# Three fused attention layers on one Trainium2 core: a step's projection or turning job placed ahead of the transposes of the probabilities on TensorE

## The chip, the cores and the metric

The kernel runs on one core of one Trainium2 chip. The metric is the device time of one execution in microseconds (us); of the kernel before, the median of 3 runs is 2838.85 us (2832.95 to 2840.29). The engines are called PE (TensorE), DVE (VectorE), ACT (ScalarE), POOL (GpSimd) and SP (SyncE). Each runs its own instruction stream in order; they meet at semaphores only.

## The reference

Four layers act one after the other on x of shape (4, 512, 512) in float32; three of them hold an attention over 512 positions:

```python
# layer 0: 16 heads of 32, q and k normalised per head
x = x + attn(_ln(x) * (scale1 + 1.0) + shift1) * gamma1
x = x + (_gelu_tanh((_ln(x) * (scale2 + 1.0) + shift2) @ Wfc1.T + bfc1) @ Wfc2.T + bfc2) * gamma2
# layer 1: 16 query heads of 32, 4 key heads, latent keys, rotary, a sparse mask
attn = jax.nn.softmax(scores, axis=-1)
y = jnp.einsum('bhts,bhsd->bhtd', attn, v_exp)
x = x + y.transpose(0, 2, 1, 3).reshape(B, T, C) @ Wo.T
# layer 2: 8 query heads of 64, one key head, rotary; then a gated MLP
ctx = jnp.einsum('bkgst,bktd->bkgsd', attn, v)
x = res + ctx @ Wo.T
x = x + (silu(h @ Wg.T) * (h @ Wu.T)) @ Wd.T
# layer 3: 8 experts of width 64, a norm and an output product
```

The change touches the attention of layers 0, 1 and 2 (called l0a, l1a and l2a in the profile), not the MLPs and not layer 3.

## The kernel before

The function `attention` is used for the three layers. A batch element is cut into "steps": step n handles one tile of 128 queries of one head, in the order group of heads (NG groups: 4, 4 and 2), query tile (4), head in the group (4). A group has 16 steps, written s = 0 to 15 below, and a batch element has 64, 64 or 32 steps. The batch elements run one after the other; the two middle ones are one loop on every engine.

The order of the work on each engine is written out by hand in a function `batch` of that engine, and only semaphores tie the engines together. In step n:

- PE multiplies probabilities of a finished query tile by V in one step of four (`weigh`, L835, into psO), computes the scores of step n+2 in l0a and n+1 in l1a and l2a (`scores`, L793 to L799, into psS), transposes the probabilities of step n-6 (`transposes`, L814, four 128x128 transposes in l0a and l2a and one or two in l1a, into one of two banks psT), and runs the step's jobs (`run`, into one of two banks psA).
- DVE takes the row minima of the negated, masked scores of step n (`minima`, L1267 and L1268), which overwrite a slot of `prob`. There are 8 slots, so it waits until PE has transposed the probabilities of step n-8.
- ACT copies the transposed probabilities of step n-7 out of psT (`pT_copy`, L992), takes the exponentials of step n (`exps`, L982), and then empties the psA banks of the jobs of step n-1 (L876, L891, L958, L973, L976 and others). Where n leaves 3 when divided by 4, the exponentials come first and the copy second, and the copy then waits for `weigh`.
- POOL multiplies four tiles of probabilities at a time by the inverse row sums (L1452, L1454).

A job is one of: "proj", "v", "kv", "far", "ck" (projections, L670 and L662), "norm" (transposes of normalised rows, L654), "q" and "k" (the transposes of queries and keys of the next group, L715), and "out" (the output product, L724). The table in `jobs` sets their steps. In l0a the q and k job of one head are both in each of the steps s = 12 to 15, and so fill both banks psA; in l1a there is one q job in each of them and one k job at s = 11, in l2a one q job in each and two k jobs at s = 11. In l0a "proj" stands at s = 2, 4, 6 and 9 (in the third group at s = 10 and 11, in the last group at s = 0 and 1 too), "v" at s = 7 and 8, "norm" at s = 7, 8, 10 and 11 of the third group, and "out" at s = 9, 10 and 11 of the first group and s = 4 of the second.

The two banks psA are taken in turn, whatever the kind of job. Before a job PE waits until the bank was emptied, in `run`:

```python
for w in freed[i]:
    pe.wait_ge(*w)
```

For q and k what it waits for is ACT's copy of the job before last. `transposes` waits for ACT's copy of step m-2 and for POOL's product of step m.

Of the kernel before, what the change touches and what calls it, by code (L numbers as in the profile page):

```python
# [362 lines left out]
def attention(nc, R, D, L, scale_g, shift_g, nxt, fetched=()):  # L363
# [13 lines left out]
    NTILE = 4 * U  # L377
# [14 lines left out]
    with ExitStack() as ctx:  # L392
# [130 lines left out]
        def s_bank(n):  # L523


            n = n % NTILE
            return NS - 2 if n == NTILE - 1 and NTILE % NS else n % NS

        def since(n):

            return next(d for d in range(1, NTILE) if s_bank(n - d) == s_bank(n))
# [62 lines left out]
        def steps(first, more):  # L594

            before = [] if first else [((kind, hg - NG, x), i) for (kind, hg, x), i in banked(first, True, False)[-1]]
            for n, todo in enumerate(banked(first, more, not more)):
                m = n - LAG  # L600
                yield n, todo, before, None if (first and m < 0) or m > NTILE + CL else m
                before = todo

        with nc.Block() as block:
# [42 lines left out]
            def _(pe):  # L647
# [129 lines left out]
                def scores(b, n, first):  # L777
                    u, j = divmod(n, 4)
                    hg, qt = divmod(u, NT)
                    g = b * NG + hg  # L780
                    if qt == 0:
                        pe.wait_ge(qT_done, 4 * g + (j + 1))
                        if is0:
                            pe.wait_ge(kT_done, 4 * g + (j + 1))
                        elif j == 0:
                            pe.wait_ge(kT_done, L.nks * (g + 1))

                    if n >= since(n) or not first:
                        pe.wait_ge(min_done, b * NTILE + (n - since(n) + 1))
                    w = L.width[qt]  # L790
                    q, out = qT[:, j, qt * P:(qt + 1) * P], psS[s_bank(n)][:, 0:w]
                    if is0:
                        mm = pe.matmul(out, q, kT[:, j, 0:w], start=True, stop=True)  # L793
                    elif is1:
                        k0 = P + (qt - 1) * WIN if qt else 0
                        mm = pe.matmul(out, q, kT[:, hg % 2, k0:k0 + w], start=True, stop=True)
                    else:
                        pe.matmul(out, q, kT[:, hg % 2 * 2, 0:w], start=True, stop=False)
                        mm = pe.matmul(out, q, kT[:, hg % 2 * 2 + 1, 0:w], start=False, stop=True)  # L799
                    mm.then_inc(s_done, 1)  # L800
# [5 lines left out]
                def transposes(b, m, first):  # L806

                    if not (first and m < 2):
                        pe.wait_ge(*pT_copied(b, m - 2))
                    pe.wait_ge(p_done, b * NTILE + (m + 1))  # L810
                    qt = m // 4 % NT
                    for c in range(L.parts[qt]):
                        k0 = (FAR if qt and c == 0 else 0) if is1 else c * P
                        mm = pe.transpose(psT[m % 2][:, c * P:(c + 1) * P], prob[:, m % NP, k0:k0 + P], R.ident[:])  # L814
                    mm.then_inc(pT_mm, 1)

                def weigh(b, u, first):

                    hg, qt = divmod(u % U, NT)
                    pe.wait_ge(*pT_copied(b, 4 * u + 3))  # L820
                    if qt == 0:
                        pe.wait_ge(v_done, (b * NG + (u // NT + 1)) * (2 if is0 else 1))
                    if qt == 0 and not (first and u == 0):
                        pe.wait_ge(oh_done, b * NG * NO + u // NT * NO)
                        pe.wait_ge(ol_done, b * NG * NO + u // NT * NO)
                    nk = L.parts[qt]
                    for c in range(nk):
                        for j in range(4):
                            o, row = divmod(j * HD, P)
                            v0 = j * HD if L.nk == 4 else 0  # L830
                            if is1 and c == 1:
                                v, rows = VF[0:FAR, hg % VS, qt - 1, :], FAR
                            else:
                                v, rows = V[:, hg % VS, qt if is1 else c, v0:v0 + HD], P
                            mm = pe.matmul(psO[o][row:row + HD, qt * P:(qt + 1) * P],  # L835
                                           v, PT[0:rows, j, c * P:(c + 1) * P],
                                           start=(c == 0), stop=(c == nk - 1))
                    mm.then_inc(pv_done, 1)

                def batch(b, first, more):  # L840
                    q_k = [(qT_done, 4 * NG * b + 4), (kT_done, L.nks * (NG * b + 1))]
                    freed[0], freed[1] = q_k, q_k
                    for n, todo, _, m in steps(first, more):
                        if m is not None and m % 4 == CL and not (first and m == CL):
                            weigh(b, m // 4 - 1, first)
                        if n + AHEAD < NTILE:
                            scores(b, n + AHEAD, first)
                        elif more and n < NTILE:
                            scores(b + 1, n + AHEAD - NTILE, False)
                        if m is not None and m < NTILE:  # L850
                            transposes(b, m, first)
                        for job, i in todo:
                            run(job, i, b, b + 1, b - 1 if n < NTILE else b)

                for n, job in enumerate(START):
                    if n == NT - PRE:
# [4 lines left out]
                for n in range(AHEAD):  # L861
                    scores(0, n, True)
                batch(0, True, True)
                with pe.Fori(1, B - 1) as b:
                    batch(b, False, True)
                batch(B - 1, False, False)


# [1498 lines left out]
```

## Time and profile before

| | |
|---|---|
| median of 3 runs | 2838.85 us |
| profiled execution | 2829.08 us |
| its span (first to last instruction) | 2827.3 us |
| PE busy | 2401.7 us (85%) |
| DVE busy | 1561.7 us (55%) |
| ACT busy | 1281.9 us (45%) |
| POOL busy | 899.4 us (32%) |
| mean granted clock of PE | 0.908 |

The profiled execution took 1.8 us more than its span and was 9.8 us below the median of the other runs. The steps of l0a lie in the span from about 125 to 770 us, those of l1a from 1213 to 1640 us, and those of l2a from 1683 to 2055 us. The MLPs and the experts lie in between and behind. Busy time counts an engine as busy from the start to the end of an instruction; on PE the ends are modelled, and the next matmul starts before the one before it has ended, so distances between starts are the better measure there.

### The profile page before, as it was taken

The numbers are of one execution on the slowest core, as the hardware profiler recorded it, in microseconds if no ns is written. First come the engines' busy times: TensorE is split into PE (matmuls) and PEld (weight loads), VectorE is DVE, ScalarE is ACT, GpSimd is POOL, SyncE is SP. The second block draws the span as 40 slices with busy tenths as digits, with TensorE's granted clock in tenths as the row PEclk, the third lists the DMA queues.
The fourth block names the chain that finished last, engine by engine and source line by source line (L and its number), as shares of the span: only waits on it lengthen the run. The fifth ranks groups of instructions, "written<-read, shape, count | busy, mean of one in ns | idle before, by whom it ended". The sixth has DMA issues, their size and how long they took to land. (4 is left out here: it accounts for less than half of the span.)

```text
span 2827.3 us, 47254 instructions
## 1 busy us (share of the span) xinstructions
PE 2401.7 (85%) x15668; PEld 1941.5 (69%) x15668; DVE 1561.7 (55%) x4469; ACT 1281.9 (45%) x3183; POOL 899.4 (32%) x988
## 2 busy tenths in 40 slices
PE   3788988898779999678788768989899999996777
PEld 1677777776567888556666557767688888885565
DVE  2777676678564343474565546566553333333866
ACT  1567676766621111276776636566531111112443
POOL 0134333342376767222332312233211212220422
PEclk7899999899889999868778689999999999997898
DMA  5100000000110000110000010000010000001000
GB/s 213 38 2 2 9 2 10 2 2 24 48 43 17 29 30 0 73 61 1 2 1 1 1 41 1 1 1 1 1 68 23 23 23 22 0 0 49 4 27 30
DMA packets 16951, 65.29 MB, mean 23 GB/s; under 512 B 3276, under 2 KB 4044, under 8 KB 11748
## 3 DMA queue, kind: packets, MB, share of 16 engines
q1 hardware_dynamic: 16740, 62.70, 6.3%
q8 instruction: 106, 1.74, 0.3%
q14 instruction: 105, 0.86, 0.1%
HBM read 57.42 MB, written 5.28 MB: 22 GB/s over the span
## 5 line engine op out<-in xcount | busy, mean ns | idle before, releaser
L1830 POOL TENSOR_TENSOR l2m_hidl<-l2m_hid,l2m_hidh 128x512 fp32r<-128x512 f32 x64 | 101.0, 1578 | 447.8 <-DVE l2m_hidh L1800 447.8
L982 ACT ACTIVATE l0a_prob<-l0a_prob,l0a_nmin 128x512 f32<-128x512 f32 x256 | 185.4, 725 | 118.6 <-DVE l0a_nmin L1268 117.3
L1695 ACT ACTIVATE l2m_gate<-l2m_psG 128x512 f32<-128x512 f32 x64 | 38.3, 599 | 437.3 <-PE l2m_psU L1626 436.3
L1452 POOL TENSOR_TENSOR l0a_prob<-l0a_prob,l0a_rinv 128x512 f32<-128x512 f32 x64 | 66.5, 1040 | 517.3 <-DVE l0a_rinv L1275 517.3
L1795 DVE TENSOR_TENSOR l2m_hid<-l2m_gate,l2m_psU 128x512 f32<-128x512 f32 x64 | 44.0, 688 | 282.3 <-ACT l2m_gate L1695 282.3
L992 ACT ACTIVATE l0a_PT<-l0a_psT 128x512 f32<-128x512 f32 x256 | 152.2, 597 | 60.3 <-PE l0a_psO L835 38.9
L1268 DVE CUSTOM_DVE_ANT_0 l0a_prob<-l0a_psS,l0a_mask 128x512 f32<-128x512 f32 x256 | 175.4, 689 | 4.6 <-PE l0a_psS L793 2.9
L1850 POOL TENSOR_TENSOR res_X<-res_X,l0m_share 128x512 f32<-128x512 f32 x128 | 162.8, 1300 | 24.9 <-DVE l0m_share L1784 23.9
L814 PE MATMUL l0a_psT<-res_ident,l0a_prob 128*128 128x128 f32 x1024 | 163.8, 285 | 3.6 <-ACT l0a_PT L992 3.2
L1699 ACT ACTIVATE l0m_hid<-l0m_psG,l0m_b1c 128x512 f32<-128x512 f32 x64 | 43.9, 690 | 265.4 <-PE l0m_psG L1626 265.4
L670 PE MATMUL l0a_psA<-l0a_wh,res_hTh 128*128 128x128 f32 (+1 forms) x512 | 151.2, 295 | 13.4 <-ACT l0a_raw L891 6.2
L793 PE MATMUL l0a_psS<-l0a_kT,l0a_qT 96*128 96x512 f32 x256 | 127.4, 499 | 41.2 <-DVE l0a_nmin L1268 31.4
L814 PEld LDWEIGHTS l0a_psT<-res_ident,l0a_prob 128*128 128x128 f32 x1024 | 134.0, 147 | 27.1 <-ACT l0a_PT L992 6.7
L814 PE MATMUL l1a_psT<-res_ident,l1a_prob 128*128 128x128 f32 x448 | 121.4, 354 | 33.9 <-ACT l1a_PT L992 32.9
L670 PE MATMUL l0a_psA<-l0a_wl,res_hTh 128*128 128x128 f32 (+1 forms) x512 | 145.1, 283 | 0.0
L670 PE MATMUL l0a_psA<-l0a_wh,res_hTl 128*128 128x128 f32 (+1 forms) x512 | 144.8, 283 | 0.0
L1454 POOL TENSOR_SCALAR l0a_prob<-l0a_prob,l0a_rinv 128x512 f32<-128x512 f32 x192 | 140.1, 746 | 0.0
L1452 POOL TENSOR_TENSOR l1a_prob<-l1a_prob,l1a_rinv 128x128 f32<-128x128 f32 (+1 forms) x64 | 32.5, 507 | 327.6 <-DVE l1a_rinv L1275 327.6
L982 ACT ACTIVATE l1a_prob<-l1a_prob,l1a_nmin 128x198 f32<-128x198 f32 (+1 forms) x256 | 114.8, 449 | 47.0 <-DVE l1a_nmin L1268 46.1
L1452 POOL TENSOR_TENSOR l2a_prob<-l2a_prob,l2a_rinv 128x512 f32<-128x512 f32 x32 | 33.9, 1059 | 300.1 <-DVE l2a_rinv L1275 300.1
L1268 DVE CUSTOM_DVE_ANT_0 l1a_prob<-l1a_psS,l1a_mask 128x198 f32<-128x198 f32 (+1 forms) x256 | 86.1, 342 | 76.5 <-issue 71.1
L1268 DVE CUSTOM_DVE_ANT_0 l2a_prob<-l2a_psS,res_zero 128x512 f32<-128x512 f32 x128 | 87.8, 687 | 69.3 <-issue 68.7
(402 smaller groups left out, 7665.7 us busy)
## 6 DMA issues: line engine op xcount, KB each, us to landing
res_l2m_stage<-in_l2m_w SPq DMA_DIRECT2D x8, 1536.0 KB, 6.4
res_l0m_stage<-in_l0m_w SPq DMA_DIRECT2D x8, 1024.0 KB, 4.8
cond_w<-in_wmod SPq DMA_DIRECT2D x6, 1024.0 KB, 7.8
res_X<-in_x SPq DMA_DIRECT2D x4, 1024.0 KB, 9.8
l0a_prob<-in_l0a_w SPq DMA_DIRECT2D x4, 1024.0 KB, 6.6
l1a_wmod<-in_wmod SPq DMA_DIRECT2D x4, 1024.0 KB, 6.1
out<-res_X SPq DMA_DIRECT2D x16, 256.0 KB, 2.0
l_stage<-in_l_w SPq DMA_DIRECT2D x3, 1024.0 KB, 7.2
```

Source lines behind the costliest of these rows:

```text
L670: mm = pe.matmul(ps[:, c0:c0 + n], l[:, k, t * P:(t + 1) * P], cols(r, k), start=(k == 0 and i == 0), stop=(k == NK - 1 and i == 2))
L793: mm = pe.matmul(out, q, kT[:, j, 0:w], start=True, stop=True)
L814: mm = pe.transpose(psT[m % 2][:, c * P:(c + 1) * P], prob[:, m % NP, k0:k0 + P], R.ident[:])
L982: act.activation(prob[:, n % NP, 0:w], src[:, 0:w], ACT.Exp, bias=nmin[:, n % NP:n % NP + 1], scale=-1.0, accum_out=ssum[:, n % NP:n % NP ...
L992: act.activation(PT[:, j, 0:w], psT[m % 2][:, 0:w], ACT.Copy).then_inc(pT_done, 1)
L1268: v.tensor_tensor_reduce(prob[:, n % NP, 0:w], psS[s_bank(n)][:, 0:w], other, -L.scale, BIG, ALU.add, ALU.min, nmin[:, n % NP:n % NP + 1]) ...
L1452: op = pool.tensor_tensor(x, x, r.to_broadcast([P, w]), ALU.mult)
L1454: op = pool.tensor_scalar(x, x, r, 1.0, ALU.mult, ALU.mult)
L1699: act.activation(hid[:, m, :], psG[m][:], ACT.Gelu_apprx_tanh, bias=b1c[:, par * MT + m:par * MT + m + 1]).then_inc(act_done, 1)
L1795: v.tensor_tensor(hid[:, m, :], gate[:, m, :], psU[m][:], ALU.mult).then_inc(hid_done, 1)
L1830: pool.tensor_tensor(hidl[:, s % 2, m, :], hid[:, m, :], f32(hidh[:, s % 2, m, :]), ALU.subtract).then_inc(hl_done, 1)
L1850: pool.tensor_tensor(x, x, share[:, t, :], ALU.add).then_inc(x_done, 1)
```

## The change

In PE's `batch` the loop over the step's jobs moves from behind `transposes` to ahead of it. Every instruction stays, with its tile, its bank and its waits; the orders of DVE, ACT, POOL and SP are the same in both kernels.

```diff
                         elif more and n < NTILE:
                             scores(b + 1, n + AHEAD - NTILE, False)
+                        for job, i in todo:
+                            run(job, i, b, b + 1, b - 1 if n < NTILE else b)
                         if m is not None and m < NTILE:
                             transposes(b, m, first)
-                        for job, i in todo:
-                            run(job, i, b, b + 1, b - 1 if n < NTILE else b)
```

The first place is on PE, l0a, the steps s = 12 to 15 of a group: psS are the scores, psT the transposed probabilities, psA0 takes the q job and psA1 the k job, psO is `weigh`. Before:

```order
L793 MATMUL l0a_psS2<-l0a_kT,l0a_qT 128x512
L814 MATMUL l0a_psT0<-res_ident,l0a_prob 128x128 x4
L715 MATMUL l0a_psA0<-res_identr,l0a_stack 96x128 x4
L715 MATMUL l0a_psA1<-res_identr,l0a_stack 96x128 x4
L793 MATMUL l0a_psS1<-l0a_kT,l0a_qT 128x512
L814 MATMUL l0a_psT1<-res_ident,l0a_prob 128x128 x4
L715 MATMUL l0a_psA0<-res_identr,l0a_stack 96x128 x4
L715 MATMUL l0a_psA1<-res_identr,l0a_stack 96x128 x4
L793 MATMUL l0a_psS0<-l0a_kT,l0a_qT 128x512
L814 MATMUL l0a_psT0<-res_ident,l0a_prob 128x128 x4
```

And now, from the same step on:

```order
L793 MATMUL l0a_psS2<-l0a_kT,l0a_qT 128x512
L715 MATMUL l0a_psA0<-res_identr,l0a_stack 96x128 x4
L715 MATMUL l0a_psA1<-res_identr,l0a_stack 96x128 x4
L814 MATMUL l0a_psT0<-res_ident,l0a_prob 128x128 x4
L793 MATMUL l0a_psS1<-l0a_kT,l0a_qT 128x512
L715 MATMUL l0a_psA0<-res_identr,l0a_stack 96x128 x4
L715 MATMUL l0a_psA1<-res_identr,l0a_stack 96x128 x4
L814 MATMUL l0a_psT1<-res_ident,l0a_prob 128x128 x4
L793 MATMUL l0a_psS0<-l0a_kT,l0a_qT 128x512
L715 MATMUL l0a_psA0<-res_identr,l0a_stack 96x128 x4
```

Between the k job of one step and the q job of the next, which waits for the copy of psA0, there still stand four transposes and one product of scores. But the transposes are now those whose copy ACT must make ahead of the copy of psA0.

The second place is on PE, l0a, the end of step s = 9 and the start of step s = 10 of a first group, where an "out" job follows a "proj" job in step 9. Before:

```order
L724 MATMUL l0a_psA0<-l0a_wh_278,l0a_oTl 128x512
L789 REGISTER_ALU
L793 MATMUL l0a_psS0<-l0a_kT,l0a_qT 128x512
L814 MATMUL l0a_psT0<-res_ident,l0a_prob 128x128 x4
L733 REGISTER_ALU
L724 MATMUL l0a_psA1<-l0a_wh_278,l0a_oTh 128x512
```

And now:

```order
L724 MATMUL l0a_psA0<-l0a_wh_278,l0a_oTl 128x512
L814 MATMUL l0a_psT1<-res_ident,l0a_prob 128x128 x4
L789 REGISTER_ALU
L793 MATMUL l0a_psS0<-l0a_kT,l0a_qT 128x512
L733 REGISTER_ALU
L724 MATMUL l0a_psA1<-l0a_wh_278,l0a_oTh 128x512
```

The transposes of step 9 (psT1) have moved from ahead of the 24 matmuls of its two jobs to behind them, and only the scores stand between them and the next job, which waits for the copy of psA1.

## Rows read from the trace of the kernel before

**Rows 1.** Busy time, instructions and granted clock in the three attention stages.

```profile
125.00:770.00 645.00, 553.62 (x5417) 469.09 (x5416) 453.35 (x1415) 438.43 (x1040) 223.82 (x271) 0.94 0.03 8
1213.00:1640.00 427.00, 350.15 (x2455) 257.56 (x2455) 243.57 (x1279) 285.36 (x1081) 122.89 (x255) 0.76 0.03 12
1683.00:2055.00 372.00, 323.59 (x2511) 263.78 (x2512) 227.91 (x670) 228.34 (x537) 110.56 (x126) 0.96 0.02 5
```

**Rows 2.** Waits, 125 to 770 us: us in total, times, longest.

```profile
PE l0a_psA L715 <- ACT l0a_qT L976: 26.5, 37, 3.2
PE l0a_psS L793 <- DVE l0a_nmin L1268: 25.3, 17, 3.3
PE l0a_psT L814 <- ACT l0a_PT L992: 3.2, 7, 0.8
...
DVE l0a_beat L1267 <- PE l0a_psT L814: 64.0, 61, 3.3
```

**Rows 3.** Waits of the transposes in l1a and l2a.

```profile
PE l1a_psT L814 <- ACT l1a_PT L992: 32.9, 53, 2.0
...
PE l2a_psT L814 <- ACT l2a_PT L992: 6.5, 11, 1.2
```

**Rows 4.** Timeline, PE and ACT, one section s = 12 to 17 in l0a.

```profile
336.57 0.78 PE L715 MATMUL l0a_psA<-res_identr,l0a_stack 128*96 128x128 f32 x8
...
337.38 0.59 ACT L992 ACTIVATE l0a_PT<-l0a_psT 128x512 f32<-128x512 f32 x1
337.50 0.60 PE L814 MATMUL l0a_psT<-res_ident,l0a_prob 128*128 128x128 f32 x4
...
337.86 0.72 ACT L982 ACTIVATE l0a_prob<-l0a_prob,l0a_nmin 128x512 f32<-128x512 f32 x1
...
338.56 0.58 ACT L976 ACTIVATE l0a_qT<-l0a_psA 96x512 fp32r<-96x512 f32 x1
...
339.04 0.59 ACT L973 ACTIVATE l0a_kT<-l0a_psA 96x512 fp32r<-96x512 f32 x1
339.20 0.95 PE L715 MATMUL l0a_psA<-res_identr,l0a_stack 128*96 128x128 f32 x8 [1.10 <-ACT l0a_qT L976]
...
339.99 0.47 PE L793 MATMUL l0a_psS<-l0a_kT,l0a_qT 96*128 96x512 f32 x1
...
341.35 0.96 PE L715 MATMUL l0a_psA<-res_identr,l0a_stack 128*96 128x128 f32 x8 [0.45 <-ACT l0a_qT L976]
...
342.24 1.08 PE L835 MATMUL l0a_psO<-l0a_PT,l0a_V 128*32 128x128 f32 x32
...
343.38 0.60 ACT L992 ACTIVATE l0a_PT<-l0a_psT 128x512 f32<-128x512 f32 x1 [0.72 <-PE l0a_psO L835]
...
344.51 0.96 PE L715 MATMUL l0a_psA<-res_identr,l0a_stack 128*96 128x128 f32 x8 [0.33 <-ACT l0a_qT L976]
...
346.49 0.60 ACT L973 ACTIVATE l0a_kT<-l0a_psA 96x512 fp32r<-96x512 f32 x1
...
347.33 0.79 PE L793 MATMUL l0a_psS<-l0a_kT,l0a_qT 96*128 96x512 f32 x1 [1.11 <-DVE l0a_nmin L1268]
```

**Rows 5.** Timeline, PE, the same steps of a later group.

```profile
421.91 1.14 PE L715 MATMUL l0a_psA<-res_identr,l0a_stack 128*96 128x128 f32 x8 [0.43 <-ACT l0a_qT L976]
...
422.98 1.94 PE L835 MATMUL l0a_psO<-l0a_PT,l0a_V 128*32 128x128 f32 x32
```

**Rows 6.** Granted clock (third column from the end) in both sections.

```profile
342.00:344.00 2.00, 2.00 (x41) 1.60 (x40) 0.60 (x3) 1.28 (x4) 1.05 (x2) 1.00 0.00 0
...
421.00:426.00 5.00, 4.56 (x50) 3.38 (x48) 2.24 (x6) 3.17 (x9) 0.84 (x1) 0.66 0.01 3
```

**Rows 7.** Timeline, l0a: a proj bank in step 10, a norm bank in step 12.

```profile
288.55 0.38 ACT L891 ACTIVATE l0a_raw<-l0a_psA 128x256 f32<-128x256 f32 x1
...
379.99 0.48 PE L715 MATMUL l0a_psA<-res_identr,l0a_stack 128*96 128x128 f32 x4 [0.92 <-ACT l0a_xn L876]
```

## The prediction, made before the changed kernel was run

> **What bounds the kernel now.** I first read the page: PE is busy 85% of the span, but that is a mean over stages, so I took the busy times of the three attention stages, the only ones the change touches [rows 1]. PE leaves 645.00 - 553.62 = 91.4 us idle in l0a, 76.9 us in l1a and 48.4 us in l2a, 217 us together; DVE and ACT are each busy for some two thirds. So no engine is the bound by itself, and the time is made by how the orders mesh. Next the waits say at what PE stands. In l0a the largest is a turning job (L715) that waits for ACT to copy the q job before it, 26.5 us in 37 waits, then the scores that wait for the minima, 25.3 us; the transposes wait for their bank only 3.2 us [rows 2]. In l1a it is the other way round: the transposes wait 32.9 us for ACT's copies, in l2a 6.5 us [rows 3]. So the change puts the jobs, which wait in l0a, ahead of the transposes, which hardly wait there.
>
> Then I read the timeline of one section with q and k jobs in l0a [rows 4]. What the reader is to see is the round of ACT: copy of psT at 337.38, exponentials 337.86, q copy 338.56, k copy 339.04, and the next copy of psT at 339.52, 2.14 us later, without a gap. PE's q job of the next step starts right behind the q copy (339.20, 341.35), after waits of 1.10 and 0.45 us. In these steps ACT is the bound and PE keeps its feed full, because the transposes (337.50) come ahead of the q and k jobs and their copy can be made while PE does the jobs.
>
> **The change, step by step.** PE only; nothing is added or removed, no DMA moves, and no queue of SP or POOL is passed. In each step with a job the job comes earlier by the transposes, 0.36 us from start to start in l0a (their end is 0.60 us after their start [rows 4]), and the transposes come later by the job's length. Who waits for the transposes: ACT's copy, with the exponentials and the job copies queued behind it on ACT; DVE's minima, which need the slot of step n-8; and `weigh`.
>
> *q and k in l0a.* I lay one section out anew from [rows 4]. The first q and k job loses nothing. Its transposes end some 0.3 us after ACT would have started their copy, so the next q job starts at about 339.5 in place of 339.20. From there a round is: q and k jobs 0.8 us (339.20 to 339.99), transposes 0.6 us to their end, copy of psT 0.48, exponentials 0.70 (337.86 to 338.56), q copy 0.64 until the next q job starts (338.56 to 339.20): 3.2 us, where it was 2.15. The third q job starts at 342.75 in place of 341.35. In the last step ACT waits for `weigh` anyway (343.38, 0.72 us), so the round grows by less: 0.8 us of jobs, 0.36 of transposes, 1.0 of `weigh`, then ACT's copy 0.5 and the q copy 0.64, 3.4 us where it was 3.16; the fourth q job starts at 346.15 in place of 344.51. Scores of the next group need the last k copy (346.49 to 347.09, scores at 347.33). That chain was 2.82 us from the q job; now it is 0.8 + 0.6 + 0.48 + 0.70 + 0.48 + 0.84 (k copy until the scores) = 3.9 us. In all 350.1 in place of 347.33, **2.8 us for a section**. There are 15 of them (four groups by four batch elements, less the first, whose jobs stand ahead of the loop). In the three at the end of a batch element I take 1.8, since all engines stand at the loop's branch anyway: 12 x 2.8 + 3 x 1.8 = **39 us**. What hid the 2.8 before was exactly the overlap of jobs and copy; nothing behind gives it back as far as I see, since DVE's minima need the transposes too and shift with them.
>
> *The clock.* After the waits of one such section the clock is 0.66, after the other 1.00 [rows 6]: (1 - 0.66) / 0.5, two thirds, of the first stretch lie at 1.2 GHz in place of 2.4. `weigh` takes 1.94 us there and 1.08 us here [rows 5], [rows 4]. With waits of some 1.7 us in place of 0.45 to 1.10 most sections should fall. Eight of the fifteen fall already; of the other seven each would pay 0.9 us for `weigh` and as much again for transposes and jobs, about 2 us. I take **15 us** (from nothing, if the clock stays as it is, to 30).
>
> The Trainium skill says on its page TensorE: Matmul & The Clock Gate (What's actually happening) that the default state is the throttled one and that activity releases it. The trace agrees: the slow `weigh` stands behind the section with the longer gaps. By that rule alone each of the fifteen sections would be slow, and the sum here is between that and nothing.
>
> *Other banks in l0a.* Wherever jobs meet in following steps the same thing happens once. At s = 10 of a first group the out job needs the bank of the proj job of s = 9; the copy, at 288.55 before [rows 7], comes now behind transposes that end 4 us later: psT copy, exponentials and proj copy (0.48 + 0.70 + 0.4) less the scores (0.33) are about 1.3 us of new wait, three times, **4 us**. In the third group v follows v plus norm (1.3 us), and the k job that already waits 0.92 us for ACT's norm copy [rows 7] waits 1.4 us more; three times, **8 us**.
>
> *l1a and l2a.* One job a step, so the bank that a job needs is that of two steps ago, whose copy is made in the ACT step ahead; PE then does job and transposes (0.8 us) while ACT is still busy with a step of over a microsecond. Nothing is lost in the run of q jobs. At the end of a run of long jobs (proj, out) ACT starts its copy late once, some 0.5 us, and hides part: **3 us**. In l2a two k jobs stand at s = 11; the q job behind them loses the cover of one set of transposes, 0.36 us, and ACT about as much: 0.7 x 7 groups = **5 us**.
>
> *Gains.* The transposes' waits in steps with a job are covered by the job now. But in l1a ACT is the one that is late, and its chain goes on at the same pace; I count 0, with all the waits of the transposes, 32.9 + 6.5 + 3.2 = 42.6 us, as what could at the very most come back.
>
> The sum is 39 + 15 + 4 + 8 + 3 + 5 = **74 us**, on the profiled 2829.1 us: 2903 us. The runs shown have their median 9.8 us above the profiled one, so I add the 74 to the median: **2913 us**.
>
> **Rivals.** (1) *The delay is given back.* DVE waits 64.0 us in l0a for the transposes [rows 2], so it often runs ahead; if PE's delay in the q and k steps leaves DVE and ACT with less to do in the next group, the 25.3 us of waits for the minima shrink, and if the clock does not fall either, of the 74 only about 74 - 15 - 25 = 34 us remain, or fewer: 2850 to 2880 us. Against it speaks that the minima themselves wait for the late transposes. 17%.
>
> (2) *DVE starves.* In l0a the minima of step n+2 may start only when the transposes of step n-6 are over, now behind the job. If DVE has no other work at hand, each of the 96 proj and v jobs (24 in each batch element) leaves its minima, 0.7 us, uncovered: 67 us more, 2980 us. Between it and my case lie those where some steps do. Against it: from s = 1 to 8 DVE works through the norms of q and k and is behind PE, so that it finds the transposes done. It decides from the point where DVE waits for psT in most of the proj steps. 13%.
>
> (3) *It gets faster.* PE would always have a job to do where it stands at the transposes now. Worked out: if a third of the 42.6 us that stand there is in steps with jobs and comes back, and the bank waits do not grow since ACT is ahead, the time is 2839 - 14 = 2825 us. It decides where ACT's copies are late by less than a job's length while psA is free: so in l1a, but not in l0a, where ACT's round has no gap [rows 4]. 5%.
> On its page Perfetto Trace Analysis (Matmul Optimizations) the Trainium skill says that matmuls should run back to back in batches, which speaks for this rival. The trace of l0a speaks against it: the job is what waits.
>
> (4) *Nothing that can be measured* (within 0.3%, some 8.5 us, about what a measurement of this kernel can tell from no change): the bank waits grow, the covered waits shrink, and the two cancel. 5%.
>
> **How the numbers follow.** My case, +46 to +110 us or 2885 to 2949 us, holds 60%. The range reaches into (1) below and towards (2) above: 2860 to 2968 us, leaving out the gain, the tie and the ends. Slower by over 0.3%: 60 + 17 + 13 = 90%; within 5%, faster 5%.
>
> **What would show it.** In l0a the wait of L715 for the q copy grows from 26.5 to 70 us or more, with single waits of 1.5 to 2 us at the second and third q job, and the section of [rows 4] goes from 10.8 us (336.57 to 347.33) to 13.5 us or more. DVE's wait for psT grows too, but the scores' wait for the minima stays near 25 us (else rival 2). The transposes' waits fall in l1a. The l0a stage grows by about 65 us, l1a and l2a by under 10 us each, the rest by nothing. The granted clock of l0a falls from 0.94 to 0.90 or so. I am wrong if the waits for the minima fall as the others rise, if the clock holds, or if l1a, whose clock is low already (0.76), moves much either way.

## The result, and the profile after

The changed kernel takes 2967.2 us (median of 4 runs, 2962.55 to 2969.53) against 2835.9 us of the kernel before (the median of its three runs and the profiled execution): the ratio is 1.0464, with a 95% interval of 1.0445 to 1.0483. It is slower by 131 us, where 74 were forecast; the time lies at the very top of the range given (2968 us), and two of the four runs lie above it. The profiled execution has a span of 2963.3 us, 136.0 us over the 2827.3 us of before.

The three stages, as in [rows 1] (us, busy PE, PEld, DVE, ACT, POOL, granted clock, DMA share, GB/s), with about the same margins around each stage:

```profile
125.00:875.00 750.00, 610.51 (x5425) 513.04 (x5424) 451.11 (x1415) 436.45 (x1040) 220.68 (x271) 0.84 0.02 7
1313.00:1760.00 447.00, 354.31 (x2457) 262.54 (x2457) 246.87 (x1287) 287.51 (x1091) 123.36 (x256) 0.76 0.03 11
1803.00:2190.00 387.00, 327.57 (x2516) 265.87 (x2516) 228.23 (x670) 226.30 (x538) 110.17 (x126) 0.95 0.01 4
```

The counts of instructions are those of before to within a few records; the window of l0a is 105 us longer. Of these, 57 us are busy time of PE at the same work, with its granted clock at 0.84 in place of 0.94, and 48 us are more idle time of PE (139.5 us where it was 91.4). To compare stages exactly I use from here on the time from the first to the last timeline row with a copy of psT into PT, good to about 0.1 us: before 620.2, 400.2 and 341.1 us, after 725.0, 419.0 and 355.7 us. So l0a has grown by 105 us, l1a by 19 and l2a by 15.

The waits of l0a (us in total, times, longest), where [rows 2] stood:

```profile
ACT l0a_PT L992 <- PE l0a_psT L814: 172.7, 111, 4.9
...
DVE l0a_beat L1267 <- PE l0a_psT L814: 146.2, 74, 4.9
...
ACT l0a_PT L992 <- PE l0a_psO L835: 73.8, 35, 3.7
...
PE l0a_psA L715 <- ACT l0a_qT L976: 57.8, 45, 3.6
...
PE l0a_psS L793 <- DVE l0a_nmin L1268: 13.6, 13, 3.2
...
PE l0a_psS L793 <- ACT l0a_kT L973: 11.0, 6, 2.8
...
PE l0a_psT L814 <- ACT l0a_PT L992: 0.9, 4, 0.3
```

And those that answer to [rows 3], of the whole execution:

```profile
ACT l2a_PT L992 <- PE l2a_psT L814: 69.1, 47, 3.6
...
ACT l1a_PT L992 <- PE l1a_psT L814: 68.4, 42, 3.6
...
PE l1a_psT L814 <- ACT l1a_PT L992: 23.2, 40, 2.0
...
PE l2a_psT L814 <- ACT l2a_PT L992: 4.8, 9, 1.2
```

ACT's waits at the same place in the kernel before, which no group of the rows ahead shows:

```profile
ACT l0a_PT L992 <- PE l0a_psT L814: 19.8, 43, 2.1
...
ACT l2a_PT L992 <- PE l2a_psT L814: 7.9, 23, 0.8
...
ACT l1a_PT L992 <- PE l1a_psT L814: 3.5, 6, 1.9
```

The reader is to see who waits now. PE's wait for its own banks (L715) has doubled from 26.5 us, but the large sums are on ACT and DVE, which stand at psT: ACT's waits for transposes in the three layers together were 31.2 us and are 310.2. PE's transposes, for their part, wait less for ACT than in [rows 3], by 9.7 us in l1a.

The section of [rows 4] in the changed kernel (timeline, PE and ACT):

```profile
368.56 0.69 PE L715 MATMUL l0a_psA<-res_identr,l0a_stack 128*96 128x128 f32 x8
...
370.25 0.71 ACT L982 ACTIVATE l0a_prob<-l0a_prob,l0a_nmin 128x512 f32<-128x512 f32 x1
...
370.95 0.58 ACT L976 ACTIVATE l0a_qT<-l0a_psA 96x512 fp32r<-96x512 f32 x1
...
371.58 0.96 PE L715 MATMUL l0a_psA<-res_identr,l0a_stack 128*96 128x128 f32 x8 [1.63 <-ACT l0a_qT L976]
...
372.38 0.62 PE L814 MATMUL l0a_psT<-res_ident,l0a_prob 128*128 128x128 f32 x4
...
373.04 0.60 ACT L992 ACTIVATE l0a_PT<-l0a_psT 128x512 f32<-128x512 f32 x1 [1.03 <-PE l0a_psT L814]
...
374.24 0.58 ACT L976 ACTIVATE l0a_qT<-l0a_psA 96x512 fp32r<-96x512 f32 x1
...
374.87 1.15 PE L715 MATMUL l0a_psA<-res_identr,l0a_stack 128*96 128x128 f32 x8 [1.63 <-ACT l0a_qT L976]
...
375.82 1.05 PE L814 MATMUL l0a_psT<-res_ident,l0a_prob 128*128 128x128 f32 x4
...
376.80 1.78 PE L835 MATMUL l0a_psO<-l0a_PT,l0a_V 128*32 128x128 f32 x32
...
378.66 0.60 ACT L992 ACTIVATE l0a_PT<-l0a_psT 128x512 f32<-128x512 f32 x1 [2.65 <-PE l0a_psO L835]
...
379.79 0.96 PE L715 MATMUL l0a_psA<-res_identr,l0a_stack 128*96 128x128 f32 x8 [0.78 <-ACT l0a_qT L976]
...
383.75 0.50 PE L793 MATMUL l0a_psS<-l0a_kT,l0a_qT 96*128 96x512 f32 x1 [1.85 <-ACT l0a_kT L973]
```

The round has two waits that feed each other. PE waits 1.63 us for a q copy; ACT makes that copy late because it first waited 1.03 us for transposes, which stand behind PE's waiting job. A round is 374.87 - 371.58 = 3.29 us; it was 2.15. From 374.87 until `weigh` is done the rows of PE are long (transposes 1.05 us against 0.62, `weigh` 1.78 against 1.08): the clock is at its lower level for most of 374.8 to 378.5 (granted 0.54). The section takes 15.19 us where it took 10.76.

To see where the rest goes I set the interval between each two score matmuls against the same interval of before, and add the growth over the 16 groups of l0a by step s (worked out from the two timelines, us):

```
s       0     1    2    3     4     5     6    7     8    9    10    11   12    13    14    15   all
grown 17.5   2.5  8.6  2.3  -2.6  -5.7  -0.5  0.7  16.8  2.3  9.9  -2.9  5.2  14.2  27.5  9.0  104.8
```

Some 84 us lie in s = 12 to 15 and the three steps behind them, and 15 of the 17 at s = 8 lie in the four third groups (3.2 to 4.3 us each).

### The profile page after: what moved, and what is told of

Same layout as the page of the kernel before. It is cut to its first block and busy times, and to the rows that moved or that the text cites. A ratio compares the mean times of both kernels' runs of the same rounds, so it can differ in the third digit from the quotient of the medians.

```text
span 2963.3 us, 47254 instructions
## 1 busy us (share of the span) xinstructions
PE 2462.4 (83%) x15668; PEld 1989.0 (67%) x15668; DVE 1561.8 (53%) x4469; ACT 1278.0 (43%) x3183; POOL 895.7 (30%) x988
## 5 line engine op out<-in xcount | busy, mean ns | idle before, releaser
L814 PE MATMUL l0a_psT<-res_ident,l0a_prob 128*128 128x128 f32 x1024 | 185.1, 312 | 1.0 <-ACT l0a_PT L992 0.9
L793 PE MATMUL l0a_psS<-l0a_kT,l0a_qT 96*128 96x512 f32 x256 | 141.2, 553 | 40.8 <-DVE l0a_nmin L1268 21.2
L1699 ACT ACTIVATE l0m_hid<-l0m_psG,l0m_b1c 128x512 f32<-128x512 f32 x64 | 43.9, 690 | 263.1 <-PE l0m_psG L1626 263.1
L670 PE MATMUL l0a_psA<-l0a_wh,res_hTl 128*128 128x128 f32 (+1 forms) x512 | 151.9, 297 | 0.0
L670 PE MATMUL l0a_psA<-l0a_wl,res_hTh 128*128 128x128 f32 (+1 forms) x512 | 151.8, 297 | 0.0
L814 PE MATMUL l1a_psT<-res_ident,l1a_prob 128*128 128x128 f32 x448 | 121.3, 355 | 24.4 <-ACT l1a_PT L992 23.2
L992 ACT ACTIVATE l1a_PT<-l1a_psT 128x256 f32<-128x256 f32 (+1 forms) x256 | 89.1, 354 | 96.6 <-PE l1a_psT L814 68.4
L670 PEld LDWEIGHTS l0a_psA<-l0a_wh,res_hTh 128*128 128x128 f32 x512 | 107.7, 210 | 31.8 <-ACT l0a_raw L891 10.5
```

The lines of the kernel that those rows point to most:

```text
L670: mm = pe.matmul(ps[:, c0:c0 + n], l[:, k, t * P:(t + 1) * P], cols(r, k), start=(k == 0 and i == 0), stop=(k == NK - 1 and i == 2))
L992: act.activation(PT[:, j, 0:w], psT[m % 2][:, 0:w], ACT.Copy).then_inc(pT_done, 1)
L1699: act.activation(hid[:, m, :], psG[m][:], ACT.Gelu_apprx_tanh, bias=b1c[:, par * MT + m:par * MT + m + 1]).then_inc(act_done, 1)
```

## The experiments

My theory behind the growth: the two banks of psA and ACT's order make the round above, and the clock falls in its waits. The rivals: every job costs a little because ACT and DVE wait for the transposes; or a layer loses by what another leaves behind. In the code below `ahead` says whether a step's jobs go ahead of its transposes on PE, `early` whether their copies stand first in ACT's step. All ratios are to the kernel before, run on the same chip.

**Where the loss lies.** Four kernels do a part of the change each:

```diff
-                        if m is not None and m < NTILE:
-                            transposes(b, m, first)
-                        for job, i in todo:
-                            run(job, i, b, b + 1, b - 1 if n < NTILE else b)
+                        ahead = ...
+                        for job, i in todo if ahead else []:
+                            run(job, i, b, b + 1, b - 1 if n < NTILE else b)
+                        if m is not None and m < NTILE:
+                            transposes(b, m, first)
+                        for job, i in [] if ahead else todo:
+                            run(job, i, b, b + 1, b - 1 if n < NTILE else b)
```

`ahead = is0 and [job[0] for job, i in todo] == ["q", "k"]`:

> The jobs stand ahead of the transposes only in the 60 steps of layer 0 that hold a q and a k job; every other step of every layer is ordered as before. The computation is whole. My theory (the loss in layer 0 is the round over the two banks: the next step's q job waits for ScalarE's copy, and the transposes, exponentials and probability copies wait behind it): from the growth of the intervals between score matmuls in the changed kernel, 73 us in these sections and 11 in the two steps behind them, so 84 us over before, about 2920 us, and TensorE's wait at the head transposes (L715) for the qT copy at 50 us or more. Rival (the loss is spread: every job ahead of the transposes delays VectorE's minima a little, 131 us over some 240 steps with jobs): these 60 steps give a quarter of it, 33 us, 2870 us.

Measured: 2898.9 us, ratio 1.0218 (1.0200 to 1.0235), 62 us over before; L715 waits 58.2 us for the q copy. Clearly above the rival's 33, and 22 under my 84.

The same with `!=` in place of `==`:

> The complement in layer 0: the jobs stand ahead of the transposes in all steps of layer 0 but those with a q and a k job; layers 1 and 2 as before. The computation is whole. My theory: 105 us of growth in layer 0 less 84, so about 21 us over before, 2857 us, most of it at the eighth step of the third groups. Rival (spread over all steps with jobs): some 70 us, 2905 us.

Measured: 2871.8 us, 1.0125 (1.0106 to 1.0144), 35 us. Between the two theories: the other jobs of l0a cost more than I had said and half of what the rival says.

`ahead = not is0`:

> The jobs stand ahead of the transposes in layers 1 and 2 alone; layer 0 as before. The computation is whole. If the losses of the layers are their own: 18 us in layer 1 and 15 in layer 2, so 33 us over before, 2869 us. Rival (these layers lost only through what layer 0 left behind, such as a colder clock or later weights): under 10 us, 2845 us.

Measured: 2871.85 us, 1.0125 (1.0108 to 1.0143), 35 us; l1a takes 420.9 us and l2a 356.9, as in the full change, l0a 617.6 as before. The losses are each layer's own. And 62.5 + 35.4 + 35.4 = 133 us: the parts add up to the whole 131.

`ahead = is0 and ("norm" in [job[0] for job, i in todo] or "norm" in last)`, where `last` holds the kinds of the step ahead:

> The jobs stand ahead of the transposes only in the steps of layer 0 that hold a norm job (12 of them, in the third group of each batch) and in the step right behind each. The computation is whole. My theory: the 4 us at the eighth step of three third groups, and up to 2 at their later steps, come from here, so 12 to 16 us over before, 2851 us; if those losses come from the v jobs without the norm jobs, nothing that can be told from before (2837 us, within 0.3%).

Measured: 2853.3 us, 1.0062 (1.0048 to 1.0076), 17 us. Half of the other jobs' loss is in 24 steps, 20 of them with jobs. (The expectation counts 12 norm jobs; the kernel has 16, since all four batch elements have them. Four of the 20 steps are q and k steps, s = 12, which e2_rest0 leaves as they were.) The changed kernel's timeline of such a place (PE and ACT; the second v job, the norm job behind it, the transposes):

```profile
400.50 0.36 ACT L958 ACTIVATE l0a_V<-l0a_psA 128x256 f32<-128x256 f32 x1
...
400.92 0.33 PE L670 MATMUL l0a_psA<-l0a_wh,res_hTh 128*128 128x128 f32 x1 [1.89 <-ACT l0a_V L958]
...
404.99 1.07 PE L654 MATMUL l0a_psA<-res_ident,l0a_xn 128*128 128x128 f32 x4
405.85 1.06 PE L814 MATMUL l0a_psT<-res_ident,l0a_prob 128*128 128x128 f32 x4
...
406.95 0.60 ACT L992 ACTIVATE l0a_PT<-l0a_psT 128x512 f32<-128x512 f32 x1 [4.69 <-PE l0a_psT L814]
```

The same pattern with longer jobs: PE waits 1.89 us for a copy that ACT makes last in its step, then does 5 us of v and norm, and only then the transposes for which ACT has stood 4.69 us. The clock falls here too, after the wait and 1.2 us of work: single matmuls go from 0.27 to 0.41 us.

One more kernel takes another part in each layer:

```diff
+                        kinds = [job[0] for job, i in todo]
+                        near = "norm" in kinds + last
+                        last = kinds
+                        if is0:
+                            ahead = not near and set(kinds) <= {"proj", "v"}
+                        elif is1:
+                            ahead = near
+                        else:
+                            ahead = set(kinds) <= {"q", "k"}
```

> The computation is whole. One kernel, another part of the change in each layer, each to be read from the length of its own stage (first to last copy of transposed probabilities; 620.2, 400.2 and 341.1 us in the trace of before). Layer 0: only proj and v jobs ahead of the transposes, but not beside a norm job. Layer 1: only the steps with a norm job and those right behind. Layer 2: only q and k jobs. From the growth tables of the changed kernel and of the runs by layer: layer 0 +7 us (the out jobs then hold 10 of what is left there), layer 1 +11 of its 20, layer 2 +11 of its 16. Rival: the loss per step with a job is about equal in all kinds (35 us over some 110 such steps in layer 0, 20 over some 120 in layer 1): layer 0 +25, layer 1 +4, layer 2 +7.

Measured: 2848.9 us, 1.0050 (1.0034 to 1.0067), 14 us; in its profiled execution, 11 us over that median, the stages grew by 14.2, 7.1 and 9.7 us. In l0a that is between the two theories (7 and 25), in l1a too and a little nearer to the rival's (11 and 4), in l2a nearer to mine (11 and 7). As the profiled execution is so far from the median, I take from it only that the proj and v jobs away from the norm jobs (66 in this kernel) cost something too, up to 14 us, and that no part comes out as a gain.

**The clock by itself.** In e1_qk's kernel, ahead of 45 of the 60 q jobs:

```diff
+                        if ahead and todo[0][0][2] > 0:
+                            pe.wait_ge(*pT_copied(b, m - 2))
+                            for c in range(4):
+                                pe.transpose(psT[m % 2][:, c * P:(c + 1) * P], R.ident[:], R.ident[:])
```

> As e1_qk (the jobs ahead of the transposes only in layer 0's steps with a q and a k job; 2898.9 us), and in 45 of those 60 steps (all but each section's first) TensorE makes four transposes of the identity into the bank that the step's own transposes will overwrite, right before the q job and its wait. They add about 45 x 0.6 us of TensorE work, which fits in the wait of 1.6 us. The computation is whole. Clock theory (a part of the 62 us is that TensorE falls to its lower clock after these waits: weigh 1.78 us in place of 1.08): layer 0's granted clock rises from 0.86 towards 0.92 and 15 to 25 us come back, 2880 us. Rival (the round alone, the clock is off the path): the time stays at 2899 within 5 us, or grows by up to 27 us where the filler doesn't fit.

Measured: 2866.7 us, 1.0109 (1.0092 to 1.0126), 32 us less than without the filler, or 31 by the two ratios. The l0a stage falls from 680.6 to 660.0 us. PE does more and is done sooner. The stretch between the same two scores of the section, from the third q and k job's step to behind `weigh`, first without and then with the filler:

```profile
358.80:364.80 6.00, 4.37 (x49) 3.22 (x47) 2.27 (x10) 2.97 (x7) 0.76 (x1) 0.55 0.00 0
```

```profile
353.80:358.40 4.60, 3.40 (x54) 2.59 (x51) 2.28 (x10) 2.97 (x7) 0.00 (x0) 1.00 0.01 4
```

With the filler (four more transposes, 0.60 us) PE is busy 1 us less, at a granted clock of 1.00 in place of 0.55. So the filler is worth 20.6 us in the l0a stage, and up to 31 by the medians (the profiled execution of e1_qk lies 11 us under its median); 660.0 - 620.2 = 39.8 us stay. But these 39.8 us are not the round at the clock of before. The `weigh` behind the third q and k job takes 1.08 us in 13 of the 15 sections with the filler, in none without it, and in 7 in the kernel before, where it takes 1.50 us or more in the other 8. The filler thus also took away slow stretches that the kernel before has. An estimate from these counts: 20.6 / 13 = 1.6 us a section, so the seven sections that became slow cost some 11 us, and the round itself 680.6 - 620.2 - 11 = 49 us. The Trainium skill says under What's actually happening on its page TensorE: Matmul & The Clock Gate that activity releases the throttle; this pair of rows agrees.

**ACT's order.** The copies of a step's jobs go first in ACT's step, ahead of the PT copy and the exponentials, at first for q and k of layer 0 (`early = is0 and len(todo) == 2 and todo[0][0][0] == "q"`), on the changed kernel and on the kernel before:

```diff
+                        early = ...
+                        for job, i in todo if early else []:
+                            run(job, i, b, b + 1)
                         if copy and (m - CL) % 4 > 0:
                             pT_copy(b, m - CL, first)
...
-                        for job, i in todo:
+                        for job, i in [] if early else todo:
                             run(job, i, b, b + 1)
```

> The changed kernel, and in ScalarE's order in layer 0 the copies of a step's q and k jobs stand ahead of the copy of transposed probabilities and of the exponentials in place of behind them. The computation is whole. My theory (the round over the two banks of psA through ScalarE's late copy is what costs): TensorE's wait at L715 for the qT copy falls from 57.8 us to under 25 and some 40 us come back, 2927 us. Rival (the cost is that the transposes come later and PT copy and exponentials wait for them): the wait moves to other places and the time stays within 15 us of 2967.

Measured: 2882.9 us, 1.0162 (1.0142 to 1.0182): 84 us come back, twice what I expected. L715's wait falls to 9.0 us and the l0a stage from 725.0 to 641.3. In the next run, with the same order on ACT and the transposes first on PE, the stage takes 598.0 us. The 43 us between them are about the 38.9 by which e2_rest0's stage grew: of the loss by q and k nothing is left.

> The kernel before, with the same edit to ScalarE's order in layer 0 alone (q and k copies first in their steps). The computation is whole. TensorE's waits for the qT copy (26.5 us) should fall to under 10; but TensorE's q and k jobs end its step, so ScalarE now waits for them ahead of its exponentials. By the first alone 2820 us; with each of 60 steps 0.5 us later, 2867 us; I expect 2845 us.

Measured: 2807.25 us, 0.9902 (0.9885 to 0.9918), 28 us faster than the kernel before. L715's wait falls from 26.5 to 6.0 us; the delay of the exponentials that I feared does not show in the time.

Then with `early = len(todo) > 0`, all jobs of all layers, on both:

> The changed kernel, and in ScalarE's order the copies of all jobs of all layers (not only q and k in layer 0) stand first in their step. The computation is whole. The q and k copies alone gave 2882.9 us. If the other jobs' loss is also that the next job waits for a late copy: layer 0 from 641 to about 615 us (the third groups give back 20), layers 1 and 2 by some 15 together, 2842 us. Rival (the other jobs lose by the transposes behind them, not by the banks): within 10 us of 2883.

Measured: 2799.4 us (2796.5 to 2805.9), 0.9873 (0.9851 to 0.9895). That is 168 us under the changed kernel, 43 under my figure and faster than the kernel before.

> The kernel before with the copies of all jobs of all layers first in ScalarE's step. The computation is whole. With the q and k copies of layer 0 alone it took 2807.3 us. The other jobs wait little for a bank in the kernel before (6 us for raw, 5 for xn), and ScalarE would now wait for the long proj and v jobs (1.3 us and more) at the end of TensorE's step ahead of its exponentials: I expect 2815 us; 2800 if the freed banks weigh more, 2850 if the exponentials' delay does.

Measured: 2813.65 us (2809.6 to 2819.1), 0.9922 (0.9899 to 0.9945), within 2 us of what I expected. The four corners:

| | ACT: job copies last | ACT: job copies first |
|---|---|---|
| PE: transposes, then jobs | 2836 us | 2814 us |
| PE: jobs, then transposes | 2967 us | 2799 us |

The change costs 131 us in one column and gains 14 in the other. The section again, with all copies first and the jobs ahead (timeline, PE and ACT):

```profile
330.11 0.58 ACT L976 ACTIVATE l0a_qT<-l0a_psA 96x512 fp32r<-96x512 f32 x1
...
330.74 0.96 PE L715 MATMUL l0a_psA<-res_identr,l0a_stack 128*96 128x128 f32 x8 [0.41 <-ACT l0a_qT L976]
331.06 0.59 ACT L992 ACTIVATE l0a_PT<-l0a_psT 128x512 f32<-128x512 f32 x1
331.54 0.62 PE L814 MATMUL l0a_psT<-res_ident,l0a_prob 128*128 128x128 f32 x4
331.54 0.72 ACT L982 ACTIVATE l0a_prob<-l0a_prob,l0a_nmin 128x512 f32<-128x512 f32 x1
...
332.89 0.96 PE L715 MATMUL l0a_psA<-res_identr,l0a_stack 128*96 128x128 f32 x8 [0.49 <-ACT l0a_qT L976]
...
334.24 1.08 PE L835 MATMUL l0a_psO<-l0a_PT,l0a_V 128*32 128x128 f32 x32
```

PE does the job, then the transposes; ACT copies the job, then the transposes, without a wait at either. The round is 332.89 - 330.74 = 2.15 us again, and `weigh` 1.08. ACT's waits for the transposes are nearly gone in the last two layers (68.4 and 69.1 us in the changed kernel):

```profile
ACT l1a_PT L992 <- PE l1a_psT L814: 3.2, 8, 0.5
...
ACT l2a_PT L992 <- PE l2a_psT L814: 1.7, 5, 0.4
```

The stages are 596.6, 398.3 and 339.8 us with the jobs ahead and 593.5, 408.7 and 342.4 with the transposes ahead: the gain is mostly the 10 us of l1a.

**Another order of ACT**, to see whether any move away from the wait would do. On the changed kernel the PT copy stands behind the exponentials in every step of layers 1 and 2:

```diff
-                        if copy and (m - CL) % 4 > 0:
+                        behind = not is0 or (m is not None and (m - CL) % 4 == 0)
+                        if copy and not behind:
                             pT_copy(b, m - CL, first)
                         if n < NTILE:
                             exps(b, n)
-                        if copy and (m - CL) % 4 == 0:
+                        if copy and behind:
                             pT_copy(b, m - CL, first)
```

> The changed kernel, and in ScalarE's order in layers 1 and 2 the copy of transposed probabilities stands behind the exponentials in every step (it did so in one of four). The computation is whole. To be read from the stages (layer 1 was 419 to 421 us with the change against 400 to 401 without, layer 2 356 to 357 against 341). Theory: these layers lose because ScalarE's copy now waits for transposes that stand behind a job (69 and 71 us of such waits against 4 and 8) and holds up the exponentials behind it; then layer 1 gets back 10 or more of its 20 us and layer 2 8 or more of its 16, about 2947 us in all. Rival (the wait is idle time that ScalarE has; the loss is TensorE's own): both stages stay within 3 us, or get longer because the probabilities' banks come free later.

Measured: 2992.1 us, 1.0562 (1.0538 to 1.0585), 25 us over the changed kernel; l1a 422.6 us, l2a 373.3. ACT's waits for the transposes fall from 68.4 to 52.1 and from 69.1 to 43.9 us, and the time gets longer. PE's waits for the same copies, now later, have grown (23.2 and 4.8 us in the changed kernel):

```profile
PE l1a_psT L814 <- ACT l1a_PT L992: 34.6, 61, 2.3
...
PE l2a_psT L814 <- ACT l2a_PT L992: 13.3, 27, 1.2
```

So the theory doesn't get its time back, and the rival named with it is borne out. It isn't refuted either: what earlier exponentials may give is mixed here with what the later PT copies cost. What gave the last two layers their time back was that the job's bank is copied before ACT turns to the transposes (420.8 and 356.8 us with q and k of layer 0 alone, 398.3 and 339.8 with all copies first). PE's waits for ACT to empty a bank psA, added up over all lines, follow it: 12.3 us in l1a and 17.7 in l2a before, 28.4 and 26.9 in the changed kernel, 3.0 and 5.2 with all copies first.

**The best of both**, copies first everywhere (`early = len(todo) > 0`), jobs ahead in layers 1 and 2 alone (`ahead = not is0`):

> ScalarE's copies of jobs first in their step in all layers; TensorE's jobs ahead of the transposes in layers 1 and 2 alone, behind them in layer 0. The computation is whole. From the stages of the two runs with all copies first (layer 0: 593.5 us with the jobs behind, 596.6 ahead; layers 1 and 2: 398.3 and 339.8 ahead, 408.7 and 342.4 behind): 3 us under the version with the jobs ahead everywhere, 2797 us, which may not be told from its 2799.4. If the gain of the change in the last two layers came through the state that layer 0 leaves, 2810 us.

Measured: 2801.3 us, 0.9890 (0.9870 to 0.9910). It can't be told from the version with the jobs ahead everywhere.

## Why the prediction was right in sign and too small

**The direction and the main mechanism held.** The round of q and k jobs was forecast at 3.2 us and measured at 3.29; L715's wait was to become 70 us or more, with single ones of 1.5 to 2 us, and fell short of that with 57.8, with 1.63 in the section. The section was to take 13.5 us or more and took 15.19. The transposes' waits in l1a fell. That the time lies inside the range is luck: it is 0.8 us under the top, less than the runs of one kernel differ by, and outside the 2885 to 2949 us that I held most likely.

Term by term, against the stages of the profiled executions (us):

| term | forecast | measured | from |
|---|---|---|---|
| q and k rounds | 39 | 39.8 | e8_fill, l0a stage 660.0 - 620.2 |
| clock behind them | 15 | 20.6 | e1_qk less e8_fill, 680.6 - 660.0 |
| other jobs of l0a | 12 (4 + 8) | 38.9 | e2_rest0, 659.1 - 620.2 |
| l1a | 3 | 20.7 | e3_l12 |
| l2a | 5 | 15.8 | e3_l12 |

That is 135.8 us against 136.0 between the two spans, closer than profiled executions that lie up to 11 us from their medians can show. The first two rows together were sized well, 54 us against 60.4. That each of them fits is in part chance: by the estimate under e8_fill they are about 49 and 11. Of the miss of 62 us, 55 are in the other three. The stages of l1a and l2a, which were to grow by under 10 us each, are what I had named as a sign of being wrong.

**The step that failed** is "wherever jobs meet in following steps the same thing happens once", and with it "one job a step, so the bank that a job needs is that of two steps ago, whose copy is made in the ACT step ahead ... nothing is lost". I looked for PE's wait for a bank and priced that alone (1.3 us a place, one set of transposes in l2a). But ACT stands at its PT copy for a result that is now behind a whole job of PE, with that job's own output ready and not copied, so both engines lose, and a job of several us makes a wait of several us (4.69 in the third group). The third groups were forecast at 8 us, for three of them, and measured at 17 for the four that there are (e4_norm; 25 in its profiled stage). The run with all copies first shows that it is this in l1a and l2a too: there the stages fall to 398.3 and 339.8 us with nothing changed on PE. I had the round of two orders in hand for q and k and did not ask for it elsewhere.

**The clock.** "From nothing to 30" is about right for the q and k sections (20.6 us by the stages, 31 by the medians), and all fifteen did fall, where most were forecast to. It was too small for the stage: the granted clock of l0a fell to 0.84 in place of 0.90, and PE's busy time grew by 57 us. What I left out is that the long jobs of the third groups run at the lower clock as well. How much of the 57 us the time has paid is not shown, since a slow stretch costs nothing where PE would have stood anyway.

**Readings and sums that were off.** That "the slow `weigh` stands behind the section with the longer gaps" is the wrong way round: the gaps ahead of the slow one are 0.93 and 0.43 us, those ahead of the fast one 1.10 and 0.45 [rows 4], [rows 5]:

```profile
419.76 0.96 PE L715 MATMUL l0a_psA<-res_identr,l0a_stack 128*96 128x128 f32 x8 [0.93 <-ACT l0a_qT L976]
```

So the rows do not show that the longer wait decides. The 15 us are also not "between that and nothing": 7 x 2 = 14 us are the price of all fifteen sections. The last round adds up to 3.3 us, not 3.4. The kernel has 86 proj and v jobs, not 96. And no run shows the smaller growth at the end of a batch element (1.8 us in place of 2.8): in e1_qk the three sections there grew by 4.9 us on average, from their s = 12 on through the three steps behind, and the twelve others by 4.5.

**The rivals.** (1) The delay given back: a part was, the scores' wait for the minima fell from 25.3 to 13.6 us, against my forecast that it would stay; but a wait for the k copies of 11.0 us took its place (that for the q copies, 9.2 us before, is 8.5). (2) DVE starves: 67 us for the proj and v jobs was far too much; in e5_parts the 66 that it moves cost 14 at most, where 0.7 us each would be 46. DVE's wait for psT did grow, from 64.0 to 146.2 us, more in the steps with q and k jobs (114.9 in e1_qk) than in the others (93.0 in e2_rest0). (3) It gets faster: not here, and it does with the other order on ACT, mostly in l1a, where this rival placed it. I had named the point from which it decides, that psA is free and ACT's copies are late by less than a job's length, but had not seen that ACT's own order sets it. On the page Perfetto Trace Analysis (Matmul Optimizations) the Trainium skill wants matmuls back to back; the four corners show that the order of the consumer decides whether a move brings them closer or apart.

What stays open: how the 39 us of the other jobs divide between norm steps (17 to 25), proj and v away from them (up to 14) and out jobs; the profiled executions of those kernels lie up to 11 us from their medians. How far the clock takes part in l1a and l2a wasn't tried.

## What to carry to other kernels

When two engines pass several results to each other in each step, what a move on one of them does is decided by the order on the other: the same move costs 131 us with one order on ACT and gains 14 with the other. To move a job on one engine is half a change: look at who takes its result and in which place, and try both places, or the two engines may wait for each other in turn. That the two orders match is no rule by itself: with the transposes first on PE, ACT is 22 us faster with the job copies first than with the matching order. In the runs here the time follows how long a finished bank psA stands before ACT empties it. Price such a move by both ends of every hand-over, not only by the engine that is moved: here the moved engine's waits for the q copy grew by 31 us and ACT's waits for the transposes by 279.

## What was not expected of the hardware

Work without use made the program faster: 180 transposes of the identity, 0.60 us for four or 27 us of rows in 45 steps, took 20.6 us off the l0a stage and 31 to 32 us off the median, because PE's granted clock stayed at the higher level (1.00 against 0.55 in the same stretch of the section, `weigh` 1.08 against 1.78 us). What PE had done before: in the changed kernel it stood 1.63 us ahead of two jobs in a row and then ran `weigh` mostly at the lower level; in the kernel with all copies first it stood 0.41 and 0.49 us and stayed at the higher. The length of the waits alone does not tell: in the kernel before, PE stood 0.93 and 0.43 us and fell, and stood 1.10 and 0.45 us and did not.
